# Nine block products in place of ten in the causal convolution of heads 4 to 31, by a shared product of kv0 + kv1

## What is computed

```python
kv = vr[:, :, :, None, :] * x2r[:, :, None, :, :]          # outer product of 8 x 8 positions
k_f = jnp.fft.rfft(k.astype(jnp.float32), n=fft_size)
y = jnp.fft.irfft(jnp.fft.rfft(kv, n=fft_size) * k_f[None, :, None, None, :], n=fft_size)[..., :L]
y = y + kv * skip
out = jnp.einsum('bhijl,bhil->bhjl', y, x1r)
```

## Time and profile before

| | |
|---|---|
| median of 3 runs | 1763.23 us |
| the profiled execution | 1760.99 us |
| its span | 1759.2 us |
| TensorE busy | 1604.6 us (91%) |
| VectorE busy | 1135.9 us (65%) |
| GpSimd busy | 824.8 us (47%) |
| ScalarE busy | 628.9 us (36%) |
| products of the convolution (L619) | 591.0 us, 1280 records for 640 products |

### The profile page before, as it was taken

The page is one execution under the profiler, slowest core; times in us unless marked ns, Lnnn a source line. Parts: engine busy times, 40 slices in busy tenths (PEclk is TensorE's granted clock), DMA queues, the critical chain, the costliest instruction groups (busy, mean ns, idle before and its releaser), DMA issues.

```text
span 1759.2 us, 27109 instructions
## 1 busy us (share of the span) xinstructions
PE 1604.6 (91%) x10758; PEld 900.8 (51%) x10758; DVE 1135.9 (65%) x1754; ACT 628.9 (36%) x1134; POOL 824.8 (47%) x621
## 2 busy tenths in 40 slices
PE   2699899898887789999999999999999999999988
PEld 2577777777773334444444444444444444444443
DVE  6798999898856796348448546634854844664521
ACT  4577778777671103202211220320221122132031
POOL 3388878788763563334334323333433432333132
PEclk9899999999998999999999999999999999999989
DMA  3654555554415130012012003001201200300000
GB/s 134 152 135 118 131 125 138 131 132 112 103 65 150 48 96 1 0 37 61 0 30 66 1 1 96 1 1 39 58 1 30 66 1 0 96 1 1 12 12 24
DMA packets 61949, 105.84 MB, mean 60 GB/s; under 512 B 7912, under 2 KB 14080, under 8 KB 61824
## 3 DMA queue, kind: packets, MB, share of 16 engines
q1 hardware_dynamic: 61728, 104.10, 22.6%
q10 hardware_dynamic: 96, 0.01, 0.0%
HBM read 50.61 MB, written 19.92 MB: 40 GB/s over the span
## 4 chain that ended last, share of the span: by engine, by line
PE 65%; DVE 20%; issue 6%; ACT 5%; POOL 3%; DMA 1%; SPq 0%; POOLq 0%; DVEq 0%; ACTq 0%
PE y L619 21%; PE gu L649 19%; PE gu L662 9%; DVE blockmax L777 3%; DVE z L961 2%; ACT fT L1341 2%; DVE oT L968 2%; POOL fnl L1506 1%; PE misc L441 1%; DVE fw_pow L840 1%; PE misc L432 1%; PE s_kq L474 1%; PE misc L599 1%; PE s_qk L453 1%; DVE fstat L997 1%
## 5 line engine op out<-in xcount | busy, mean ns | idle before, releaser
L619 PE MATMUL y<-kv,toep 128*128 128x512 f32 x1280 | 591.0, 598 | 8.7 <-DVE z L961 8.3
L619 PEld LDWEIGHTS y<-kv,toep 128*128 128x128 f32 x1280 | 235.7, 191 | 262.3 <-issue 215.8
L1493 POOL TENSOR_TENSOR fuL<-fu,fuH 128x512 f16<-128x512 f32 x96 | 110.9, 1155 | 383.7 <-ACT fuH L1322 383.7
L1424 POOL TENSOR_TENSOR pL<-pT,pH 128x768 f16<-128x768 f32 x128 | 220.1, 1721 | 89.1 <-PE pv L508 36.7
L984 DVE SCALAR_TENSOR_TENSOR fu<-gu,cols,sil 128x512 f32<-128x512 f32 x96 | 71.9, 749 | 222.0 <-PE gu L649 126.6
L961 DVE TENSOR_TENSOR z<-y,cT 128x512 f32<-128x512 f32 x256 | 174.7, 683 | 46.2 <-PE y L619 45.5
L649 PE MATMUL gu<-fT,wg 128*128 128x512 f16 x768 | 183.1, 382 | 3.2 <-ACT fT L1341 3.2
L649 PE MATMUL gu<-fT,wu 128*128 128x512 f16 x768 | 181.4, 379 | 0.0
L968 DVE TENSOR_REDUCE oT<-z 128x64 f32<-128x512 f32 x256 | 175.6, 686 | 8.8
L1176 ACT ACTIVATE pT<-s_kq,ws 128x768 f32<-128x768 f32 x128 | 115.2, 900 | 103.4 <-PE s_kq L488 103.4
L662 PE MATMUL gu<-wd,fuH 128*128 128x512 f16 x384 | 145.5, 379 | 5.2 <-POOL fuL L1493 5.2
(11 more groups left out here) (179 smaller groups left out, 3128.9 us busy)
## 6 DMA issues: line engine op xcount, KB each, us to landing
pack<-qkhl SPq DMA_DIRECT2D x256, 128.0 KB, 2.6
x_sb<-in_x SPq DMA_DIRECT2D x16, 512.0 KB, 4.8
c_sb<-in_ctx SPq DMA_DIRECT2D x32, 256.0 KB, 5.0
hankel<-in_L_xattn_k SPq DMA_DIRECT2D x32, 256.0 KB, 5.1
x_grp<-x_scratch SPq DMA_DIRECT2D x32, 256.0 KB, 3.9
out_y<-yo SPq DMA_DIRECT2D x32, 256.0 KB, 2.9
x_scratch<-x_sb SPq DMA_DIRECT2D x15, 512.0 KB, 3.0
wraw<-in_L_attn_w_qkv SPq DMA_DIRECT2D x3, 1024.0 KB, 8.6
```

Source lines behind the costliest of these rows:

```text
L619: made = T.matmul(y_bank[n % 2][:], toep[h % 2][:, (lb - kb) * P:(lb - kb + 1) * P], kv[LB * (h % 2) + kb][:, half * HB:(half + 1) * HB, : ...
L1424: G.tensor_tensor(pL[n % 2][:], pT[n % NP][:], pH[n % NP][:], ALU.subtract).then_inc(low_done, 1)
L1493: G.tensor_tensor(fuL[:, ib, :], fu[n % 2][:], fuH[:, ib, :], ALU.subtract).then_inc(f_fl, 1)
```

## The change

For heads 4 to 31, rows 2 and 3 of the block matrix both hold T2 times kv: row 2 has T2 kv0 + T1 kv1 + T0 kv2, row 3 has T3 kv0 + T2 kv1 + T1 kv2 + T0 kv3. With S = T2 (kv0 + kv1), row 2 is S + (T1 - T2) kv1 + T0 kv2, and row 3 is S + (T3 - T2) kv0 + T1 kv2 + T0 kv3. That is 9 block products in place of 10, on two halves: 18 products per head for 20.

- TensorE: `mix_shared` makes S for one half in slots 2 and 3 into a bank of the ring `gu`; slots 4 and 5 hold 2 products for 3, slots 6 and 7 hold 3 for 4.
- ScalarE: `copy_shared` copies S to SBUF, first thing in slots 2 and 3.
- VectorE: for slots 4 to 7 `weigh_sum` first adds S to the bank (into z, this now releases the bank), then multiplies z by cT in place, then sums: three operations for two.
- GpSimd: in slot 6 it makes the two differences of taps (`toep_less`, 256 columns), in slot 7 the sum kv0 + kv1 (`kv01`, 1024 columns), ahead of kv blocks 2 and 3, and it waits there for VectorE's kv block 1.
- Memory: `d_raw` and `d_pow` share their space with what comes after them (`fuH` and `fuL`), and ScalarE waits once for `d_taken`.

```diff
@@ -199,6 +199,9 @@
         kv = [q(f"kv{i}", [P, B, M_POS, M_POS], F32) for i in range(2 * LB)]
+        kv01 = q("kv01", [P, B, M_POS, M_POS], F32)
+        shared = [q(f"shared{i}", [P, HALF], F32) for i in range(2)]
+        toep_less = [q(f"toep_less{i}", [P, 2, P], F32) for i in range(2)]
         z = [q(f"z{i}", [P, HB, M_POS, M_POS], F32) for i in range(2)]
@@ -207,11 +210,13 @@
         fu = [q(f"fu{i}", [P, GN], F32) for i in range(2)]
+        with ExitStack() as down_prep:
+            d_raw = [sb(down_prep, f"d_raw{i}", [P, C], F32) for i in range(3)]
+            d_pow = [sb(down_prep, f"d_pow{i}", [P, C], F32) for i in range(2)]
...
         yo = [q(f"yo{i}", [P, C], F32) for i in range(2)]
-        d_raw = [q(f"d_raw{i}", [P, C], F32) for i in range(3)]
-        d_pow = [q(f"d_pow{i}", [P, C], F32) for i in range(2)]
@@ -381,6 +387,11 @@
+        SHARED_FROM, SHARED_AT = GROUP, (2, 3)
+        def n_shared(h, half):
+            return 2 * (h - SHARED_FROM) + half + 1
         BOUND_AT = (0, 6), (1, 4), (2, 4)
@@ -606,19 +617,42 @@
+            def tap(h, d):
+                return toep[h % 2][:, d * P:(d + 1) * P]
+            def keys_values(h, kb, half):
+                if kb < 2:
+                    w.wait_ge(m_kv, 2 * h + kb + 1)
+                else:
+                    w.wait_ge(m_kvp, 2 * h + kb - 1)
+                return kv[LB * (h % 2) + kb][:, half * HB:(half + 1) * HB, :, :].rearrange("p b j i -> p (b j i)")
+            def mix_shared(h, half):
+                bank = gu.take(("shared", h, half), w, (m_shc, n_shared(h, half)))
+                w.wait_ge(m_kvs, h - SHARED_FROM + 1)
+                T.matmul(bank[:], tap(h, 2),
+                         kv01[:, half * HB:(half + 1) * HB, :, :].rearrange("p b j i -> p (b j i)"),
+                         start=True, stop=True).then_inc(m_sh, 1)
...
                 lb, half, n = s // 2, s % 2, 2 * LB * h + s
+                to = y_bank[n % 2][:]
                 w.wait_ge(m_toep, h + 1)
...
                     w.wait_ge(m_zm, n - 1)
-                for kb in range(lb + 1):
-                    if kb < 2:
-                        w.wait_ge(m_kv, 2 * h + kb + 1)
-                    else:
-                        w.wait_ge(m_kvp, 2 * h + kb - 1)
-                    made = T.matmul(y_bank[n % 2][:], toep[h % 2][:, (lb - kb) * P:(lb - kb + 1) * P],
-                                    kv[LB * (h % 2) + kb][:, half * HB:(half + 1) * HB, :, :].rearrange("p b j i -> p (b j i)"),
-                                    start=kb == 0, stop=kb == lb)
+                if h < SHARED_FROM or lb < 2:
+                    for kb in range(lb + 1):
+                        made = T.matmul(to, tap(h, lb - kb), keys_values(h, kb, half), start=kb == 0, stop=kb == lb)
+                elif lb == 2:
+                    w.wait_ge(m_less, h - SHARED_FROM + 1)
+                    T.matmul(to, toep_less[h % 2][:, 0, :], keys_values(h, 1, half), start=True, stop=False)
+                    made = T.matmul(to, tap(h, 0), keys_values(h, 2, half), start=False, stop=True)
+                else:
+                    T.matmul(to, toep_less[h % 2][:, 1, :], keys_values(h, 0, half), start=True, stop=False)
+                    T.matmul(to, tap(h, 1), keys_values(h, 2, half), start=False, stop=False)
+                    made = T.matmul(to, tap(h, 0), keys_values(h, 3, half), start=False, stop=True)
                 made.then_inc(m_y, 1)
@@ -680,6 +714,8 @@
                     mix(h, s)
+                    if h >= SHARED_FROM and s in SHARED_AT:
+                        mix_shared(h, s - SHARED_AT[0])
                     if s == 2 and h >= 1:
@@ -958,11 +994,18 @@
                 w.wait_ge(m_cT, h + 1)
-                V.tensor_tensor(
-                    z[n % 2][:], y_bank[n % 2][:].rearrange("p (b j i) -> p b j i", b=HB, i=M_POS),
-                    cT[h % 2][:, lb, own].rearrange("p (b i) -> p b i", b=HB).unsqueeze(2).broadcast_to([P, HB, M_POS, M_POS]),
-                    ALU.mult).then_inc(m_zm, 1)
-                w.wait_ge(m_zm, n + 1)
+                y = y_bank[n % 2][:].rearrange("p (b j i) -> p b j i", b=HB, i=M_POS)
+                weight = cT[h % 2][:, lb, own].rearrange("p (b i) -> p b i", b=HB).unsqueeze(2).broadcast_to([P, HB, M_POS, M_POS])
+                if h < SHARED_FROM or lb < 2:
+                    V.tensor_tensor(z[n % 2][:], y, weight, ALU.mult).then_inc(m_zm, 1)
+                    w.wait_ge(m_zm, n + 1)
+                else:
+                    w.wait_ge(m_shc, n_shared(h, half))
+                    V.tensor_tensor(z[n % 2][:], y, shared[half][:].rearrange("p (b j i) -> p b j i", b=HB, i=M_POS),
+                                    ALU.add).then_inc(m_zm, 1)
+                    w.wait_ge(m_zm, n + 1)
+                    chain.step(V.tensor_tensor(z[n % 2][:], z[n % 2][:], weight, ALU.mult))
+                    chain.wait()
                 if h >= 2:
@@ -1306,6 +1349,12 @@
+            def copy_shared(h, half):
+                w.wait_ge(m_sh, n_shared(h, half))
+                if h > SHARED_FROM:
+                    w.wait_ge(m_zm, 2 * LB * (h - 1) + 7 + half)
+                S.activation(shared[half][:], gu.of["shared", h, half][:], ACT.Copy).then_inc(m_shc, 1)
@@ -1356,6 +1407,8 @@
                 for s in range(2 * LB):
+                    if h >= SHARED_FROM and s in SHARED_AT:
+                        copy_shared(h, s - SHARED_AT[0])
                     for gi, f in FEED[h, s]:
@@ -1470,7 +1523,12 @@
                     G.tensor_tensor(rstd, rstd, minus_half[:, 0:1], ALU.pow).then_inc(m_rstd, 1)
-                elif k in (7, 8):
+                if k == 7 and h >= SHARED_FROM:
+                    w.wait_ge(m_kv, 2 * h + 2)
+                    if h > SHARED_FROM:
+                        w.wait_ge(m_sh, n_shared(h - 1, 1))
+                    G.tensor_tensor(kv01[:], kv[LB * (h % 2)][:], kv[LB * (h % 2) + 1][:], ALU.add).then_inc(m_kvs, 1)
+                if k in (7, 8):
                     lb = k - 5
@@ -1481,6 +1539,13 @@
                         ALU.mult).then_inc(m_kvp, 1)
+                if k == 6 and h >= SHARED_FROM:
+                    w.wait_ge(m_toep, h + 1)
+                    if h >= SHARED_FROM + 2:
+                        w.wait_ge(m_y, 2 * LB * (h - 1))
+                    taps = toep[h % 2][:].rearrange("p (d c) -> p d c", d=LB)
+                    G.tensor_tensor(toep_less[h % 2][:], taps[:, 1::2, :], taps[:, 2:3, :].broadcast_to([P, 2, P]),
+                                    ALU.subtract).then_inc(m_less, 1)
                 if k == 8:
```

More of the change, by code:

```diff
@@ L255, in decoder_kernel @@
         m_u, m_w, m_wx, m_res = signal("m_u"), signal("m_w"), signal("m_wx"), signal("m_res")
-        m_kv, m_kvp = signal("m_kv"), signal("m_kvp")
+        m_kv, m_kvp, m_kvs = signal("m_kv"), signal("m_kvp"), signal("m_kvs")
+        m_less, m_sh, m_shc = signal("m_less"), signal("m_sh"), signal("m_shc")
         m_y, m_zm, m_z, m_o, m_x2 = signal("m_y"), signal("m_zm"), signal("m_z"), signal("m_o"), signal("m_x2")
@@ L1321, in high_fu @@
                     w.wait_ge(f_down, GROUP * gi)
+                else:
+                    w.wait_ge(d_taken, IB)
                 S.activation(fuH[:, ib, :], fu[n % 2][:], ACT.Copy).then_inc(f_fh, 1)
```

## The result

| | before | changed |
|---|---|---|
| median of 4 runs, us | 1765.01 (1763.21 to 1766.99) | 1808.23 (1805.78 to 1811.64) |
| profiled execution: time / span, us | 1760.99 / 1759.2 | 1805.78 / 1804.1 |
| mean granted clock | 0.979 | 0.963 |
| `fT` of one group to the next | 146.08 | 153.29 |

The changed kernel takes 1.0246 times the time of before [1.0223, 1.0269]: slower, as forecast, but by 43 us where 21 were forecast, and beyond the range's upper end of 1800 us.

The account below looks back on a forecast made before the run. TensorE was taken to bound the covered slots, VectorE's queue the end of each bare stretch. Six periods at +4.0 us (+24), +1.5 first and -4.4 last give +21 us on 1763.2: 1784 us, range 1762 to 1800 us.

Parts of the forecast that it names:

- The bound of the bare stretch: Bare stretch, 937 to 975 us in heads 11 and 12: VectorE is busy 34.65 of 38 us; its queue sets the end.
- (a): Bare stretch: slot 4's shorter product ends the down step, and with it VectorE's wait, earlier: -0.86 us.
- (b): Bare stretch: six VectorE additions stand ahead of the last `fnh`, 0.71 us each: +4.26 us.
- (c): Bare stretch: GpSimd must wait, so VectorE's two kv blocks run alone: -2.11 us.
- kv blocks of VectorE all near 1.2 us: Sign expected in the profile after: VectorE's kv blocks take about 1.2 us; before, two took 2.88 and 1.65 us.
- (d): Bare stretch: products with cT, now reading two SBUF tiles, wait for GpSimd's work: +2.7 us, bounds 0 and 6.7.
- The clock: Bare stretch: TensorE's pauses bring one fall of the granted clock to 1.2 GHz: +1.7 us, bounds 0 and +3.4.
- rival 2: The granted clock falls twice, also at the transposes: another 1.7 us in each of seven stretches, 1796 us; chance 0.16.
- Covered slots: Slots where TensorE has no idle time: net -2 products, -1.72 us per period; the S copies cost nothing.
- The sum: Per period -1.72 + 4.0 + 1.7 = +4.0 us, six make +24; first stretch +1.5, end -4.4; total +21 us.
- rival 1: The granted clock stays up in the bare stretch: +2.3 us per period, 1774 us; chance 0.20.
- rival 3: The product in place is not held and the clock stays: bare stretch +1.3 us, total 1757 us; chance 0.13.

Follow-up runs that it names:

- experiment 1: Changed kernel, but sharing T2 only in heads 4k + 1 and 4k + 2: 1747.99 us, 0.9909 of the kernel before.
- experiment 2: Changed kernel, but sharing T2 only in heads 4k + 3 and 4k: 1817.09 us, 1.0308 of the kernel before.
- experiment 3: Changed kernel, with S added in place in the PSUM bank, so the product with cT has one SBUF input: 1772.11 us, 1.0046 of the kernel before.
- experiment 5: Changed kernel, with VectorE's addition of S left out and the other engines' work kept: 1749.09 us, 0.9913 of the kernel before.
- experiment 7: Kernel before, plus a wait that puts GpSimd's kv blocks 2 and 3 behind VectorE's kv block 1: 1763.54 us, 1.0000 of the kernel before.
- experiment 4: Changed kernel, plus unread float16 products on TensorE in the bare stretches' pauses: 1787.49 us, 1.0133 of the kernel before.
- experiment 8: Changed kernel with both experiment 3's addition in PSUM and experiment 4's filler products: 1776.42 us, 1.0070 of the kernel before.
- experiment 6: Changed kernel, with SyncE issuing the next head's `c_sb` and `hankel` loads ahead of the output store: 1798.63 us, 1.0205 of the kernel before.
- experiment 9: Experiment 1, with the first down step's first half waiting only for the blocks it reads: 1732.62 us, 0.9824 of the kernel before.
- experiment 10: Kernel before, with only the finer wait of the first down step: 1756.01 us, 0.9958 of the kernel before.

## Why the prediction was right and wrong

- **The bound of the bare stretch: right.** VectorE's queue sets its end. Experiments 1, 2, 3 and 5 show it from four sides: without sharing there it stays at 42.19 us, the loss comes with the heads that reach into it, and with the clock up the six additions alone make the difference between 39.97 and 43.72 us.
- **(a) -0.86: right.** `yo` starts 4.08 us after slot 4's product, before 4.94.
- **(b) +4.26: right.** The additions start 0.72 us ahead of the products behind them, and without them a bare stretch is 3.75 us shorter.
- **(c) -2.11: right.** VectorE's kv blocks in slots 5 and 6 of head 11 take 1.22 us each. In the kernel before this would be worth nothing by itself (experiment 7), since TensorE arrives no earlier; in the changed kernel TensorE waits for VectorE there, and it counts. What did not come is "kv blocks of VectorE all near 1.2 us": in head 12 they fall beside the last `fnl` and take 2.18 and 2.17 us, of which the first stood there before (2.17) and the second comes behind the last `fnh`.
- **(d) +2.7: the mechanism right.** In slots 4 to 7 of head 11 the products took 1.04, 0.69, 1.75 and 1.00 us, and 0.93 in slot 5 of head 12: held for 2.0 us together, where 2.7 stood, the longest (slot 6) beside GpSimd's sum as foreseen. The rule of the Trainium skill that the prediction drew on ("SBUF — State Buffer", section "SBUF: two separate sides") holds in this case: 1056 ns on the mean with two tiles in SBUF, 692 with one (experiment 3). The 38 of the 112 products with two that have no work of GpSimd beside them take 691 to 693 ns. By the durations (a) to (d) are -0.86 + 4.3 - 2.1 + 2.0 = +3.3, where the bare stretch shows +3.0 and the sum was +4.0; the mis-sized term is (d). By experiments 4 and 8 (d) is worth 1.3 us of the stretch.
- **The clock: the first step that failed.** "I expect one fall per bare stretch, +1.7 us". There were two in each of the six, together 3.5 us (experiment 4): 1.8 at `turn_back` and 1.6 at the transposes. So the price of a fall was right and the number of falls wrong; rival 2 had the true mechanism. The forecast named a pause of about 3 us before the transposes itself and gave it no fall; it was 2.70 us, and the fall came. And I added holds and clock as separate terms: experiment 3 shows that they hang together, since without holds the pauses at slot 1 and at the transposes are shorter (0.91 us in place of 1.96, and at most 1.75 in place of 2.70), half of the falls are gone and the rest cost 1.2 us in two stretches and nothing in the others. Removing the holds gave 36 us, where their own length in six bare stretches is some 12.
- **Covered slots: the second step that failed.** "VectorE and ScalarE have the room" is true of both (VectorE is busy for 22.56 of 37 us and 22.80 of 39 us there), and the -1.72 us still came out as +0.5. I counted products and not what TensorE meets when it has fewer. Slot 5's saved product only brings it sooner to the `fuL` that the down step waits for (0.31 us of waiting became 1.17, just the 0.86 saved); and GpSimd's added sum delays a `yo`, behind whose store SyncE's load of c_sb stands. I followed VectorE's queue and not SyncE's. Experiment 6 sizes the second at 7 to 10 us, experiments 1 and 9 take the first away (15.4 us, of which the kernel before gains 6.8 too, experiment 10).
- **The sum:** forecast 4.0 per period = -1.72 + 4.0 + 1.7; measured 0.5 + 3.4 + 3.5 = 7.4 in heads 11 to 15, 7.1 on the mean of the six. The first stretch took +2.5 (1.5), the end -2.5 (-4.4), and 2.1 us lie ahead of all shared heads, which no term had.
- **Rivals 1 and 3** are out: the clock fell, the product was held. But the bare stretch of rival 3 is in experiment 3: with no product held and the clock up it grew by 1.5 us where rival 3 had +1.3. The kernel still takes 1772 us and not 1757, mostly since the covered slots don't give their -1.72, and for the rest by the falls that are left.

What stays open: what decides whether given pauses bring a fall. Pauses of 0.99 and 0.91 us were followed by one in two of experiment 3's six bare stretches and by none in the other four. Nor is the 2.1 us ahead of the shared heads explained.

## What to carry to other kernels

An exchange of work between engines is priced by place: a product saved is worth its time only where its engine ends the stretch, and an operation added is free only where the receiving engine has room, so make the exchange per slot and not for a whole loop (here 28 of 56 products: -1.8% with a finer wait, 0.4 of it by the wait alone, where all 56 gave +2.5%). Where TensorE is left with pauses, price its clock together with whatever makes them longer. When an engine arrives earlier, look for what it will wait for next, and for loads that stand in a queue behind a store of a late engine.

## What the runs showed of the hardware

- Two pauses of 0.98 and 1.96 us with one product between were followed by a fall of the granted clock to 1.2 GHz, though neither is long; a single pause of 1.88 us in the kernel before was not the earlier trace rows. Pauses of 0.99 and 0.91 us were in two cases of six (experiment 3).
- The low clock lasted 3.4 us at the transposes, and behind slot 0 it lasted 7 us in four stretches and 3.4 in two; what it cost at `turn_back` was nearly the same.
- VectorE's product of two SBUF tiles (128x512, float32) takes 0.69 us alone and up to 2.17 us beside GpSimd's work; with one input in PSUM it took 692 ns on the mean in 112.
- GpSimd's sum of two tiles of 1024 columns takes 2.35 us without VectorE's products of two SBUF tiles (experiment 3), and 2.57 us on the mean over 28 with them.
